# One full 32-bit matmul per product in place of three on rounded parts, in the local pass of a two-layer graph network

## The reference

```python
def _gcn_conv(x, W, b, src, dst, dinv):
    h = x @ W
    norm = dinv[src] * dinv[dst]
    agg = segment_sum(h[src] * norm[:, None], dst, N)
    return agg + (dinv * dinv)[:, None] * h + b
x = _l2norm(_gcn_conv(node_embedding, W1, b1))        # 128 -> 256, "first"
def f(z):
    z1 = _l2norm(_gcn_conv(z, Wf1, bf1))              # 256 -> 256, "mid"
    return _gcn_conv(z1, Wf2, bf2) + z                # 256 -> 256, "end"
k1 = f(x); k2 = f(x + 0.5*k1); k3 = f(x + 0.5*k2); k4 = f(x + k3)
x = x + (k1 + 2*k2 + 2*k3 + k4) / 6
return _gcn_conv(x, W2, b2)                           # 256 -> 128, "last"
```

## Time and profile before

| | |
|---|---|
| median of 2 runs | 7419.17 us (7414.28 to 7424.07) |
| span of the profiled execution | 7463.9 us |
| mean granted TensorE clock | 0.938 of 2.4 GHz |
| TensorE matmul, weight load | 6262.2 us (84%), 5197.7 us (70%) |
| VectorE, ScalarE, GpSimd | 6114.0 (82%), 3838.3 (51%), 4840.9 us (65%) |

### The profile page before, as it was taken

The page is one execution under the profiler, slowest core; times in us unless marked ns, Lnnn a source line. Parts: engine busy times, 40 slices in busy tenths (PEclk is TensorE's granted clock), DMA queues, the critical chain, the costliest instruction groups (busy, mean ns, idle before and its releaser), DMA issues. The chain is left out here.

```text
span 7463.9 us, 156875 instructions
## 1 busy us (share of the span) xinstructions
PE 6262.2 (84%) x37260; PEld 5197.7 (70%) x37260; DVE 6114.0 (82%) x15796; ACT 3838.3 (51%) x10696; POOL 4840.9 (65%) x5469
## 2 busy tenths in 40 slices
PE   7699889899999657989989998999888765877776
PEld 3588888888889436867766676667666554865664
DVE  8588778787888777889879977997799887878887
ACT  6466666666666576733661166116622233654443
POOL 0488888888873576855776577657744565546665
PEclk8799999999999899999999999999999998988998
DMA  0365555554444466879779977997799765543432
GB/s 2 102 165 161 161 160 158 162 161 152 146 145 152 146 190 199 247 257 297 229 223 332 329 226 224 331 327 228 230 385 387 259 186 151 152 138 119 125 123 86
DMA packets 981268, 1483.74 MB, mean 199 GB/s; under 512 B 156967, under 2 KB 450705, under 8 KB 980647
## 3 DMA queue, kind: packets, MB, share of 16 engines
q1 hardware_dynamic: 685479, 922.39, 37.2%
q0 software_dynamic: 141504, 309.42, 16.2%
q10 hardware_dynamic: 153664, 244.12, 9.0%
HBM read 902.58 MB, written 573.11 MB: 198 GB/s over the span
## 5 line engine op out<-in xcount | busy, mean ns | idle before, releaser
L1336 PE MATMUL bank<-c_rows,sums_all 128*128 128x256 f32 (+1 forms) x3920 | 1320.9, 420 | 550.5 <-DVE c_rows L1487 304.3
L751 PE MATMUL bank<-wf_w,c_xt 128*128 128x256 f32 x6272 | 1615.0, 381 | 2.0 <-DVE y L1545 2.0
L1381 ACT ACTIVATE c_xt<-bank 128x512 f32<-128x512 f32 (+1 forms) x980 | 556.8, 568 | 1586.6 <-issue 831.0
L1307 POOL DMA_INDIRECT c_rows<-t_tab,src_pair x784 | 870.2, 1110 | 705.6 <-PE bank L1336 546.2
L1336 PEld LDWEIGHTS bank<-c_rows,sums_all 128*128 128x128 f32 x3920 | 633.9, 194 | 984.7 <-DVE c_rows L1487 478.7
L751 PEld LDWEIGHTS bank<-wf_w,c_xt 128*128 128x128 f32 x6272 | 1133.7, 191 | 127.0 <-ACT c_xt L1381 3.5
L1487 DVE SCALAR_TENSOR_TENSOR c_rows<-bank,carry,c_rows 32x256 f32<-32x256 f32 (+1 forms) x1950 | 913.7, 469 | 274.3 <-PE bank L1336 117.6
L1307 POOL DMA_INDIRECT c_rows<-z_tab,src_pair x784 | 770.7, 983 | 293.3 <-issue 189.5
L1085 DVE TENSOR_TENSOR lx_lo<-bank,lx_hi 128x512 fp32r<-128x512 f32 (+1 forms) x1000 | 658.6, 659 | 260.6 <-ACT lx_hi L1030 217.4
L1030 ACT ACTIVATE lx_hi<-bank 128x512 fp32r<-128x512 f32 (+1 forms) x1000 | 569.4, 572 | 580.4 <-PE bank L999 418.6
L741 PE MATMUL bank<-wf_hi,lx_hi 128*128 128x256 f32 x3200 | 725.0, 309 | 62.7 <-issue 49.4
(11 more groups left out here) (333 smaller groups left out, 14629.2 us busy)
## 6 DMA issues: line engine op xcount, KB each, us to landing
c_z<-z_tab SPq DMA_DIRECT2D x882, 256.0 KB
z_tab<-lz SPq DMA_DIRECT2D x400, 256.0 KB
t_tab<-lt SPq DMA_DIRECT2D x400, 256.0 KB
z_tab<-y ACTq DMA_DIRECT2D x392, 256.0 KB
c_own<-z_tab SPq DMA_DIRECT2D x392, 256.0 KB
t_tab<-y ACTq DMA_DIRECT2D x392, 256.0 KB
c_own<-t_tab SPq DMA_DIRECT2D x392, 256.0 KB
fl_x<-x_tab SPq DMA_DIRECT2D x396, 128.0 KB
```

Of the source, the lines that this page charges most:

```text
L751: last = nc.tensor.matmul(out, x(k), w[:, k, :], start=(k == 0), stop=(k == ks - 1 and not bias))
L1307: pool.indirect_dma_start(out=rows[:, s, i, 0:win], out_offset=None, in_=source, in_offset=bass.IndirectOffsetOnAxis(ap=m["src_i"][:, t:t ...
L1336: nc.tensor.matmul(psum[s % 2][:, i * win:(i + 1) * win], sums[:, j * 2 + i, :], rows[:, s, i, 0:win], start=True, stop=True).then_inc(S[" ...
L1381: nc.scalar.activation(xt[:, s % 2].rearrange("p k n -> p (k n)")[:, 0:n], psum[2 + s % 2][:, 0:n], ACT.Copy).then_inc(S["copied"], 1)
```

## The change

Each product of the local pass becomes one matmul per 128 rows of the contraction on full 32-bit words (`full_product`). ScalarE's copy writes a plain 32-bit tile `lxt`, VectorE's `low` is gone, and TensorE's waits for the low part become waits for the copy. The preparation no longer splits the four weights into parts; the bias parts stay. Lines that only rename are left out.

```diff
@@ split_weights
             def _(act):
-                act.wait_ge(S["weights_in"], 64)
-                for n, (name, ks, width, _) in enumerate(parts):
-                    last = nc.scalar.activation(m[name + "_hi"][:, 0:ks, :], m[name + "_w"][:], ACT.Copy)
-                last.then_inc(S["w_hi"], 1)
...
             def _(dve):
-                for n, (name, ks, width, _) in enumerate(parts):
-                    nc.vector.tensor_tensor(m[name + "_lo"][:, 0:ks, :], m[name + "_w"][:],
-                                            m[name + "_hi"][:, 0:ks, :].bitcast(F32), ALU.subtract)
@@ local_pass
-        x_hi = sb("lx_hi", [P, 4, 2, H2], F32R)
-        x_lo = sb("lx_lo", [P, 4, 2, H2], F32R)
+        xt = sb("lxt", [P, 4, 2, H2])
@@ turn
-                        pe.wait_ge(S["low"], ph.at("low", *prev))
+                        pe.wait_ge(S["copied"], ph.at("copied", *prev))
@@ multiply
-                    pe.wait_ge(S["high"], ph.at("high", b, q))
-                    pe.wait_ge(S["low"], ph.at("low", b, q))
+                    pe.wait_ge(S["copied"], ph.at("copied", b, q))
...
-                        last = product(nc, psum[4 + n][:, i * width:(i + 1) * width],
-                                       lambda k: x_hi[:, n, k, i * P:(i + 1) * P],
-                                       lambda k: x_lo[:, n, k, i * P:(i + 1) * P],
-                                       m[w + "_hi"], m[w + "_lo"], ks,
-                                       (m["ones_r"], m["bf2_parts"]) if kind[c] == "end" else None)
+                        last = full_product(nc, psum[4 + n][:, i * width:(i + 1) * width],
+                                            lambda k: xt[:, n, k, i * P:(i + 1) * P], m[w + "_w"], ks,
+                                            (m["ones_r"][:], m["bf2_parts"][:]) if kind[c] == "end" else None)
@@ vector
-                def low(b, q, odd):
-                    n = H2 if layer[q] == 0 else 2 * H2
-                    k = bank(b, q)
-                    dve.wait_ge(S["high"], ph.at("high", b, q))
-                    v.tensor_tensor(x_lo[:, k].rearrange("p k n -> p (k n)")[:, 0:n], psum[k][:, 0:n],
-                                    x_hi[:, k].rearrange("p k n -> p (k n)")[:, 0:n].bitcast(F32),
-                                    ALU.subtract).then_inc(S["low"], 1)
-                staggered(dve, blocks, Q, early, [(6, normalise), (1, low), (3, add_rest), (3, take), (0, build)])
+                staggered(dve, blocks, Q, early, [(6, normalise), (3, add_rest), (3, take), (0, build)])
```

More of the change, by code:

```diff
@@ L266, in gnn_kernel @@
         early("dst_f", [P, TE])
-        for name, ks, width in (("w1", 1, H2), ("wf1", 2, H2), ("wf2", 2, H2), ("w2", 2, D)):
-            early(name + "_hi", [P, ks, width], F32R)
-            early(name + "_lo", [P, ks, width], F32R)
         early("ones_r", [P, P], F32R)
@@ L700, in _ @@
                     sp.dma_start(m[name][:], a[key].partition_broadcast(P)).then_inc(S["biases_in"], 16)
+                sp.wait_ge(S["weights_in"], 64)
                 sp.wait_ge(S["biases_in"], 64)
@@ L713, in _ @@
             def _(dve):
-                dve.wait_ge(S["weights_in"], 64)
-                dve.wait_ge(S["w_hi"], 1)
                 dve.wait_ge(S["biases_in"], 64)
                 nc.vector.tensor_scalar(not_one[:], m["ident"][:, 1:2], -1.0, 1.0, ALU.mult, ALU.add)
-                for n, (name, ks, width, _) in enumerate(parts):
-                    nc.vector.tensor_tensor(m[name + "_lo"][:, 0:ks, :], m[name + "_w"][:],
-                                            m[name + "_hi"][:, 0:ks, :].bitcast(F32), ALU.subtract)
                 nc.vector.tensor_scalar(m["ones_r"][:], m["ident"][:], 0.0, 1.0, ALU.mult, ALU.add)
@@ L733, in _ @@
                                                b_rest[:], ALU.mult, ALU.add)
[L736 to L745, removed]
 def full_product(nc, out, x, w, ks, bias=None):
@@ L818, in local_pass @@
         rates = {
-            "turned": one, "high": one, "low": one, "product": one, "taken": one,
+            "turned": one, "copied": one, "product": one, "taken": one,
             "rest_set": [[0, 0, 0, 0, 1, 0, 1, 0, 3, 1][layer[q]] for q in range(Q)],
@@ L1022, in _, with copy @@
             def _(act):
-                def high(b, q, odd):
+                def copy(b, q, odd):
                     n = H2 if layer[q] == 0 else 2 * H2
@@ L1029, in high @@
                         act.wait_ge(S["product"], ph.at("product", *prev))
-                    nc.scalar.activation(x_hi[:, k].rearrange("p k n -> p (k n)")[:, 0:n], psum[k][:, 0:n],
-                                         ACT.Copy).then_inc(S["high"], 1)
+                    nc.scalar.activation(xt[:, k].rearrange("p k n -> p (k n)")[:, 0:n], psum[k][:, 0:n],
+                                         ACT.Copy).then_inc(S["copied"], 1)
                 def begin_rest(b, q, odd):
@@ L1065, in square @@
                     last.then_inc(S["squared"], 1)
-                staggered(act, blocks, Q, early, [(0, high), (6, scale), (1, begin_rest), (4, square)])
+                staggered(act, blocks, Q, early, [(0, copy), (6, scale), (1, begin_rest), (4, square)])
             @block.vector
```

## The result

| | before | after |
|---|---|---|
| median (range) | 7419.17 us (7414.28 to 7424.07) | 7494.91 us (7494.51 to 7495.31) |
| ratio, 95% interval | | 1.0102 (1.0073 to 1.0131) |
| span of the profiled execution | 7463.9 us | 7492.4 us |
| table block: mean of 20 blocks with tables | 88.8 us | 92.4 us |
| last full block, behind the last table | 81.2 us | 82.7 us |

The change costs 76 us, 1.0%. The forecast was +101 us, and 7494.91 lies in its range. The blocks are measured between the first gathers that POOL issues in each.

The account below looks back on a forecast made before the run. POOL and PE were taken to bound each local-pass block in turns. 21 table blocks at +4.5 (+95), +8 behind the last table and -1.9 in the preparation made +101 us on 7419, so 7520, range 7455 to 7615.

Parts of the forecast that it names:

- A pair of 4.57 us: Local pass: PE's time for a "mid" and an "end" unit, forecast to grow from 3.99 to 4.57 us.
- Stretch B: PE's part of a block, from unit 8' to the end of unit 33's product: 56.05 us growing by 7.3 to 63.3.
- Stretch A: POOL's part of a block, up to the next block's unit 8' on PE: 34.2 us before, forecast 32.5, bounds 31.9 to 35.5.
- T0: Start mark of a block: end of POOL's first inverse behind the block's first gather, that of unit 28; 90.35 us apart before.
- POOL's queue is the same: First part of the block: POOL's gathers, tables and inverses unchanged, the inverse of 0' ending 30.8 us in.
- The lead of 2.2 us: Block's end, at unit 36: POOL's inverse of unit 28 ends about 2.2 us before PE is ready, where it came 0.1 after.
- The block: One table block of the local pass: 32.5 + 63.3 - 2.2 = 93.6 us; +4.5 taken, bounds +1.8 and +9.5.
- Behind the last table +8: Local pass after the tables end: some 5 of PE's 8.1 us won back, +3 x 2.7 blocks = +8 us.
- The preparation -1.9: Before the local pass: the weights' low parts leave VectorE's path, 1.9 us saved.
- PE pays in full: Rival, local pass: stalls stay, so each block grows by its whole 8.1 us; +196 us, 7615; chance 0.16.
- The low clock: Rival: PE's clock stays at 0.50 through the products up to 7', +3 us per block beside the forecast, 7583; chance 0.14.
- POOL's floor: Rival: PE runs so far ahead that only POOL's 85 us count; blocks shrink by 3.5 us, 7351; chance 0.08.

Follow-up runs that it names:

- e1: The kernel after, with VectorE still making an unused low part per unit and PE waiting for it; 7554.99 us, 1.0176 of before.
- e2: The kernel before without low parts of the activations: each product's third matmul reads the high part again; 7383.98 us, 0.9942 of before.
- e3: The kernel before with one matmul (high by high) per product in place of three and no low parts; 7328.55 us, 0.9880 of before.
- e6: The kernel after with six of a block's 36 table DMAs moved away from units 28 to 33 to other units; 7384.07 us, 0.9952 of before.

## Why the prediction was right, step by step

**A pair of 4.57 us.** Measured 4.56, so the two prices from the rows (0.12 a part, 0.217 an instruction of a full product) hold in the local pass. The two forms differ by 7.64 us a block, where the rows gave 8.1. The page's figure of 0.109 per pass (the Trainium skill, "TensorE: Matmul & The Clock Gate", Back-to-back issue gap, which gives it for a matmul by itself) would have given 7600 by the prediction's estimate.

**Stretch B +7.3 us.** Measured +6.3 in this block (62.3 against 56.05), +6.5 in the mean of the table blocks: a little oversized.

**Stretch A to T0 + 32.5, bounds 31.9 to 35.5.** The direction is right, the size is not: 31.25 here, 30.6 in the mean, below the lower bound. Two steps failed. The first is what ends the stretch: the forecast took PE, from a late product of 2' on and half at 0.50. That holds in this block only, and with other terms: the product of 2' starts at 961.05 = T0 + 25.0, not at 22.9, and PE needs 6.3 us from there. In the other 19 blocks it is what the forecast had as its lower bound, POOL's inverse of 0' and a scale behind it: 29.6 + 1.0 in the mean, where it had 30.8 + 1.1. The second is "POOL's queue is the same". Its instructions are the same, but in these two blocks the inverse of 0' starts at T0 + 29.0 (965.11) in place of T0 + 30.5: single DMAs, clamps and powers in between are 0.1 to 0.4 us shorter, and a wait of 0.42 is gone. In the mean it starts 0.8 us sooner, T0 + 28.9 in place of 29.7. The prediction named two waits "for the low part" too, of which one was the loop's turn and stayed (3.37 us).

**The lead of 2.2 us.** Measured 1.0: T0 comes 1.0 us before unit 36, and ScalarE's scale waits 1.53 in place of 3.58. POOL does get ahead in stretch B, but it is held to PE's pace by ScalarE's squares as late as 1020.22, 8 us before the next T0. The scale ends less than 0.1 us before PE takes its result, so POOL comes in time with nothing to spare. The term was over 1 us too good.

**The block.** 31.25 + 62.3 - 1.0 = 92.55 us (92.57 from T0 to T0), where 93.6 was forecast. Per table block +3.6 in place of +4.5, so 75 in place of 95 over 21 blocks. By stretches in the mean that is -2.0 in A, +6.5 in B and -0.9 at unit 36.

**Behind the last table +8.** Measured +1.6 in the last full block and -8.1 in the drain. The block was read rightly (PE's new work fills its idle time), but by more. The drain was left out of the sum. There the last four pairs run down the layers 5 to 9 with nothing beside them. The low part was one of the steps of each of these units, and without it the drain is 14.9 us shorter with full products (e1 to after) and 18.4 with parts (before to e2).

**The preparation -1.9.** Measured -2.0.

**The sum.** The forecast was 25 us high: 20 in the table blocks and 14.5 behind the last table, less 9 us behind the local pass, which it put at nothing. So part of its nearness is luck: in the block, too, A and B came out about 1 us shorter each and the lead about 1 us smaller, which partly cancels. Two of its bounds do not come out as written. The low terms add to 31.9 + 63.3 - 3.6 = 91.6, which is +1.3 against the one block and +3.1 against the mean, where +1.8 stands; and +9.5 over 21 blocks is 7618, above the 7585 that it gives for the forecast alone and above the top of its range.

**The rivals.** *PE pays in full* (7615) would have needed the waits of before to stay; even with VectorE's old work (e1) the price was 131 us. The rule that looks for the limit in the most-contended engine (the Trainium skill, "Perfetto Trace Analysis", Identifying the Most-Contended Engine) agrees with the blocks behind the last table, where PE is busy throughout and the block follows its work. Read as the prediction reads it, that the time goes with that engine, it fails in table blocks: in e2 PE is the busiest engine (902 of 1000 us, POOL 810), e3 takes a third of that away, and the block moves by 1.2 us. *The low clock* did not spread: two windows of 2 us at 0.50 with 0.75 to 0.90 beside them, and 1.00 from 958 to 968; in 1000 to 1200 it is 0.99 (0.95 before). *POOL's floor* (85 us) is there, at 87; after did not reach it, since unit 8' starts at T0 + 31 and not 24. e6 moved it to T0 + 23 to 26, and then the block came down to the floor as that rival's condition said.

## What to carry to other kernels

When two engines set the pace by turns within one period, cost an edit stretch by stretch: work added to the engine of one stretch is paid there, however idle that engine stands in the other, and relief for a third engine can end in the queue that holds the other stretch (here 0.6 of 6 us a block). Before paying for a dearer instruction, look at which fixed-order queue makes the costly engine wait; here moving six DMA issues per block gave 111 us with full products and 38 with parts, and left 4 us between the two forms. And sum the run-down at the end of a pipeline by itself: a step taken out of a unit's chain is worth more there than in any full block.

## What was not expected of the hardware

- A name behind a wait can be wrong for a reason that no engine shows: waits of 0.9 to 3.9 us at one unit in every second block were put down now to a low part and now to "issue" in one trace, to "issue" in two that have no low part, and were gone when PE's loop was written out.
- GpSimd's instructions vary with what runs beside them: the same first inverse took 1.15 us before and 1.02 after. The same 18 DMAs with the clamps and powers among them, from T0 to the inverse of 0', are busy for 24.0 us in the mean before and in e1, where VectorE makes low parts, and for 23.4 and 23.3 in e2 and after, where it does not. So it goes with VectorE's low parts and not with the form of product; by what way, no run shows.
- Taking work from PE lowered its granted clock: 0.82 in e3 where it is busy for 614 of 1000 us, 0.95 before and 0.99 in e6. Where another engine holds PE up, idle time and a lower clock came together.
